# SyncE's issue of the expert blocks' quarter transfers: unrolled program against a loop of six blocks on the engine

## The chip, the cores and the metric

One core of one Trainium2 chip runs one program. The metric is the time on the device in microseconds (us), the median of several runs. All five engines work side by side, each through its own sequence of instructions; they meet at semaphores. SyncE (SP in the profile) computes nothing: it issues DMA transfers.

## The reference, cut to what matters

The computation is one layer over x of 32 sequences of 256 rows of 512 numbers: a cross attention with 16 heads whose result is added to x, and then a routed feed-forward product that is added as well. Only the second part is touched:

```python
scores = jnp.einsum('sp,tp->st', pe, jnp.sign(tile_sigs))
idx = jnp.argmax(scores, axis=-1)                    # one of 8 experts for each position
y_all = jnp.einsum('bsd,tod->bsto', x, W) + b
out = jnp.take_along_axis(y_all, idx4, axis=2)[:, :, 0]
x = x + out                                          # the x in the product is normalized
```

The expert depends on the position (0 to 255) alone, so all 32 sequences send the same position to the same expert.

## The kernel before, in words

Until about 700 us the kernel runs the attention, tile by tile. It leaves two arrays in HBM: `y_scratch` (the sum so far, plus the expert's bias) and `x_scratch` (the same rows normalized, in four column quarters). Then the expert stage begins. The 256 positions are sorted by expert and padded to 70 blocks (`NR`) of four positions (`PB`); four positions times 32 sequences are the 128 rows of a block. Which four positions block j holds is known only at run time; they stand in the small tile `position_of`.

For each block j five engines work:

- SP, in `gather_quarters`: it waits until the slot of `xq` is free (`x2t_ready` at least j - 5; there are R = 6 slots), reads the four positions of the block into registers (L1645, one TENSOR_LOAD), and issues four transfers of 64 KB from `x_scratch` (L1649). The source address of each comes from a register, which takes a FUSED_REGOPS and a MOVE ahead of each DMA. In the program before, j is a number of the program's text: the 70 blocks stand one behind the other, 280 transfers in all.
- DVE: it transposes the block from `xq` to `x2t` (L1698, two slots), computes the low part of x (L1703), and in `finish` adds the product to the gathered rows of y (L1711). A `finish` waits for the product, for the gathered rows and for an earlier scatter.
- ACT: it rounds `x2t` to its high part (L1688).
- PE: 12 matmuls of 128x512 a block (L1747), into two PSUM buffers in turn; a block waits for the `finish` of two blocks earlier (`y2_ready`). PE already runs its 70 blocks as a first turn of six in the program's text, a loop of ten turns of six blocks (`pe.Fori`, L1768), and four blocks at the end.
- POOL: an indirect gather of y rows (L1663), five blocks ahead, and an indirect scatter of the result (L1669), one of each a block, 256 KB each.

The order on each engine is written out by hand. Nothing but SP's own program and the freed slot holds back a quarter transfer.

Of the kernel before, what the change touches and what calls it, by code (L numbers as in the profile page):

```python
# [31 lines left out]
P = 128  # L32
B, S, DM = 32, 256, 512
# [11 lines left out]
PB = P // B  # L45
NR = (S + NE * (PB - 1)) // PB
# [18 lines left out]
def wait(eng, sem, value):  # L65

    if isinstance(value, int) and value <= 0:
        return
    eng.wait_ge(sem, value)
# [82 lines left out]
def kernel_program(nc, x, x_t, ctx_t, mask, pad, wq, wk, wv, wo, sigs_t, wf, bf, ident_d, choose_d, slots_d, place_d, pe_t, out):  # L152
# [4 lines left out]
    x_quarters = nc.dram_tensor("x_scratch", (KC * B, S, P), F32, kind="Internal").ap()  # L157
    top = ExitStack()
    with top:
        def sb(name, shape, dt=F32, stack=top):  # L160
            return stack.enter_context(nc.sbuf_tensor(name, shape, dt))

        def sem(name):
            return top.enter_context(nc.semaphore(name))
# [15 lines left out]
        position_of = sb("position_of", [1, NR, PB], I32)  # L180
# [1443 lines left out]
        R = 6  # L1624
        xq = sb("xq", [P, R, DM])
# [7 lines left out]
        quartered = [sem(f"quartered_{r}") for r in range(R)]  # L1633
        x2t_ready = sem("x2t_ready")
# [3 lines left out]
        y2_ready = sem("y2_ready")  # L1638
        scattered = [sem(f"scattered_{r}") for r in range(3)]

        def gather_quarters(eng, j, quarters):

            r = j % R
            wait(eng, x2t_ready, j + 1 - R)
            _, at = nc.values_load_multi_w_load_instructions(  # L1645
                position_of[0:1, j, quarters.start:quarters.stop], engines=[eng.engine], min_val=0, max_val=S - 1,
                skip_runtime_bounds_check_because="a position comes from a one-hot product with the numbers 0 to 255")
            for s, n in zip(at, quarters):
                eng.dma_start(xq[:, r, n * P:(n + 1) * P],  # L1649
                              x_quarters[:, bass.ds(s, 1), :].rearrange("p a f -> p (a f)")).then_inc(quartered[r], 16)  # L1650

        def experts_sync(sp):
            sp.wait_ge(positions_known, 1)
            for j in range(NR):
                gather_quarters(sp, j, range(PB))

        def experts_gpsimd(pool):
            last_row = pool.to_reg(B * S - 1)
# [115 lines left out]
        with nc.Block() as block:  # L1774
# [33 lines left out]
            @block.sync  # L1808
            def _(sp):
                either(sp, short_sync(sp, SHORT), full_sync)  # L1810
                experts_sync(sp)
# [92 lines left out]
```

## Time and profile before

| | |
|---|---|
| median of 3 runs | 945.48 us (943.81 to 946.06) |
| profiled execution, its own time | 945.56 us |
| its span in the trace | 943.7 us |
| granted TensorE clock, mean | 0.985 |
| busy: PE, PEld, DVE, POOL, ACT | 93%, 74%, 76%, 68%, 46% |
| SP's queue (q1) | 104.69 MB, 35.5% of 16 DMA engines' span |
| POOL's queue (q0) | 35.66 MB, 11.8% |

The span is what the trace covers; about 1.9 us of the execution's own time lie around it. Register, branch, semaphore and DMA-issuing instructions are not counted as busy. In rows an engine's name with a q is its sequencer (SPq, PEldq); "issue" in a chain is time in which the engine waited for nothing that the profile shows. The expert stage is the last quarter of the span, from 700 us on.

### The profile page before, as it was taken

How to read it: one execution, taken by the hardware profiler on the slowest of the kernel's cores; microseconds unless marked ns; L12 is line 12 of the kernel's file. 1: busy time of each engine (PE TensorE's matmuls, PEld its weight loads, DVE VectorE, ACT ScalarE, POOL GpSimd, SP SyncE). 2: the span in 40 equal slices, each digit the busy share in tenths (PEclk: the TensorE clock that was granted, in tenths of full speed). 3: DMA queues.
4: the chain of work that ended last, by engine and by line, in shares of the span. 5: the costliest groups of instructions: out<-in, count | busy, mean ns of one | idle time of the engine just before them, and what ended most of it. 6: DMA issues, size and time to landing. Idle time of an engine off the chain costs nothing.

```text
span 943.7 us, 16943 instructions
## 1 busy us (share of the span) xinstructions
PE 879.9 (93%) x5430; PEld 700.6 (74%) x5431; DVE 715.6 (76%) x1021; ACT 432.5 (46%) x762; POOL 640.2 (68%) x833
## 2 busy tenths in 40 slices
PE   6999999999999999999999999999927888888986
PEld 4788887887888788788878878887715666666765
DVE  5899778788887878888788888887757666666664
ACT  5545555565555556455545655553561212111211
POOL 3687777586676858767685866765674666666764
PEclk9999999999999999999999999999968999999999
DMA  9513242424324242532433243322876777778883
GB/s 347 179 35 121 71 145 82 125 78 148 117 75 144 83 125 69 158 97 96 133 93 125 69 158 82 110 70 79 290 249 199 237 236 239 242 242 243 249 247 116
DMA packets 123123, 141.59 MB, mean 150 GB/s; under 512 B 16128, under 2 KB 89376, under 8 KB 120992
## 3 DMA queue, kind: packets, MB, share of 16 engines
q1 hardware_dynamic: 111296, 104.69, 35.5%
q0 software_dynamic: 11360, 35.66, 11.8%
q8 instruction: 42, 0.69, 0.3%
q14 instruction: 41, 0.34, 0.1%
q10 hardware_dynamic: 384, 0.21, 0.1%
HBM read 90.18 MB, written 51.90 MB: 151 GB/s over the span
## 4 chain that ended last, share of the span: by engine, by line
PE 85%; issue 4%; SPq 3%; DMA 3%; DVE 2%; POOL 2%; ACT 1%; DVEq 0%; POOLq 0%; ACTq 0%
PE pS L1458 29%; PE pA L1458 19%; PE pA L1747 15%; PE pS L1524 7%; PE pA L1547 7%; PE pT L1535 6%; SPq L1649 2%; DMA x_scratch<-y_normal 1%; DMA xq<-x_scratch 1%; PE pS L1484 1%; DVE y L1711 1%; POOL wf_hl L321 1%; POOL y_biased L1057 1%; DVE wf_hl L321 1%; DVE x2t L1698 0%
## 5 line engine op out<-in xcount | busy, mean ns | idle before, releaser
L1747 PE MATMUL pA<-wf_hl,x_hi 128*128 x560 | 144.6, 401 | 40.6 <-DVE y L1711 22.3
L1747 PEld LDWEIGHTS pA<-wf_hl,x_hi 128*128 128x128 f32 x560 | 105.6, 191 | 71.0 <-issue 50.3
L1301 DVE TENSOR_TENSOR s<-pS,bias 128x1024 f32<-128x1024 f32 x57 | 69.3, 1217 | 75.9 <-PE pS L1524 75.9
L1688 ACT CAST x_hi<-x2t 128x512 fp32r<-128x512 f32 x70 | 43.4, 621 | 182.0 <-PE pA L1747 106.3
L1072 POOL TENSOR_TENSOR s<-s,row 128x1024 f32<-128x1024 f32 x64 | 121.7, 1902 | 4.5 <-DVE row L1321 4.5
L1669 POOL DMA_INDIRECT out_dram<-y,scatter_rows x70 | 79.6, 1138 | 63.7 <-DVE y L1711 48.8
L1188 ACT CAST ot_hi<-pA 128x512 fp32r<-128x512 f32 x64 | 37.6, 587 | 180.3 <-PE pA L1547 180.3
L1458 PE MATMUL pA<-wo_hi,ot_hi 128*128 128x512 f32 x256 | 108.8, 425 | 2.9 <-DVE ot_lo L1325 2.9
L1048 POOL TENSOR_SCALAR y_mom<-y_mom 128x1 f32<-128x1 f32 x64 | 13.8, 216 | 143.6 <-DVE y_mom L1341 142.1
L1458 PE MATMUL pS<-xt_hi,wq_hi 128*128 128x512 f32 x256 | 105.0, 410 | 2.3 <-DVE wq_lo L1361 2.3
L1458 PE MATMUL pA<-wo_hi,ot_lo 128*128 128x512 f32 x256 | 101.5, 396 | 0.0
L1458 PE MATMUL pA<-wo_lo,ot_hi 128*128 128x512 f32 x256 | 101.4, 396 | 0.0
L1458 PE MATMUL pS<-xt_hi,wq_lo 128*128 128x512 f32 x256 | 100.7, 393 | 0.0
L1458 PE MATMUL pS<-xt_lo,wq_hi 128*128 128x512 f32 x256 | 100.4, 392 | 0.0
L1032 POOL TENSOR_TENSOR xt_lo<-xt_raw,xt_hi 128x512 fp32r<-128x512 f32 x64 | 94.4, 1505 | 6.7 <-ACT xt_hi L1144 6.7
L1310 DVE SCALAR_TENSOR_TENSOR s<-row,s 128x1024 f32<-128x1024 f32 x57 | 95.2, 1670 | 1.9
L1663 POOL DMA_INDIRECT yg<-y_scratch,gather_rows x70 | 71.2, 1017 | 25.1 <-issue 16.8
L1711 DVE TENSOR_TENSOR y<-pA,yg 128x512 f32<-128x512 f32 x70 | 47.2, 674 | 51.6 <-PE pA L1747 48.7
L1057 POOL TENSOR_TENSOR y_biased<-y,bias_at 128x512 f32<-128x512 f32 x64 | 82.0, 1282 | 2.7 <-DMA x_scratch<-y_normal 2.7
L1316 DVE TENSOR_REDUCE row<-s 128x16 f32<-128x1024 f32 x64 | 76.0, 1188 | 3.2 <-ACT s L1178 2.9
L1178 ACT ACTIVATE s<-s,rstd 128x1024 f32<-128x1024 f32 x64 | 73.9, 1155 | 9.1 <-DVE s L1310 8.8
L1747 PE MATMUL pA<-wf_hl,x_lo 128*128 x280 | 75.1, 390 | 2.1 <-DVE x_lo L1703 2.1
(131 smaller groups left out, 1935.8 us busy)
## 6 DMA issues: line engine op xcount, KB each, us to landing
xq<-x_scratch SPq DMA_DIRECT2D x280, 64.0 KB
xt_raw<-in_x_t SPq DMA_DIRECT2D x16, 1024.0 KB, 6.8
x<-in_x SPq DMA_DIRECT2D x64, 256.0 KB, 3.2
y_scratch<-y_biased SPq DMA_DIRECT2D x64, 256.0 KB, 2.1
x_scratch<-y_normal SPq DMA_DIRECT2D x64, 256.0 KB, 2.8
wf_hl<-in_wf SPq DMA_DIRECT2D x8, 1024.0 KB, 8.5
ctx_raw<-in_ctx_t SPq DMA_DIRECT2D x32, 128.0 KB, 2.8
mask_early<-in_mask SPq DMA_DIRECT2D x1, 1536.0 KB, 11.3
```

Of the source, the lines that this page charges most:

```text
L1032: pool.tensor_tensor(h.xt_lo[:, k, :], h.xt_raw[:, k, :], h.xt_hi[:, k, :].bitcast(F32), ALU.subtract)\
L1057: pool.tensor_tensor(y_biased[:, t % 2, :], y_sb[:, t % 2, 0:DM], bias_at[:, t % 2, :], ALU.add)\
L1072: pool.tensor_tensor(p, p, h.row[:, t % h.c, 3, :].unsqueeze(2).broadcast_to([P, H, BK]), ALU.mult)\
L1178: act.activation(p, p, ACT.Exp, scale=h.rstd[:, t % h.c, 2:3]).then_inc(exp_ready, 1)
L1301: dve.tensor_tensor(h.s_sb[:, t % h.c, :].rearrange("p (h k) -> p h k", h=H), pS[:, 0, :].rearrange("p (h k) -> p h k", h=H), h.bias[:, t ...
L1310: dve.scalar_tensor_tensor(p, h.row[:, t % h.c, 0, :].unsqueeze(2).broadcast_to([P, H, BK]), FLOOR, p, ALU.max, ALU.subtract).then_inc(shi ...
L1316: dve.tensor_reduce(row[:, 1, :], h.s_sb[:, t % h.c, :].rearrange("p (h k) -> p h k", h=H), AX.X, ALU.add).then_inc(sum_ready, 1)
L1458: mm = pe.matmul(dst, lhs[a], rhs[b], start=(k == 0 and n == 0), stop=(k == KC - 1 and n == 2))
L1524: mm = pe.matmul(pS[:, 0, g2 * 512 + m * P:g2 * 512 + (m + 1) * P], h.qt[half, g % 2, m, q * P:(q + 1) * P], h.kd[half, g % 2, q // 2, m, ...
L1663: pool.indirect_dma_start(yg[:, r, :], None, y_rows, bass.IndirectOffsetOnAxis(ap=gather_rows[:, j:j + 1], axis=0))\
L1669: pool.indirect_dma_start(out, bass.IndirectOffsetOnAxis(ap=scatter_rows[:, j:j + 1], axis=0), y2[:, j % 3, :], None, bounds_check=last_ro ...
L1747: return pe.matmul(pA[:, r % 2, :], rows[:, r % 2, c * P:(c + 1) * P], w, start=first, stop=last)
```

## The change

`gather_quarters` takes a turn k and a place n in it, j = 6k + n, in place of j. Turn 0 (blocks 0 to 5) and the last four blocks (66 to 69) stay in the program's text; turns 1 to 10 (blocks 6 to 65) are a loop on SyncE whose body holds six blocks. In the body k is a register. So the address of the four positions and the value that `x2t_ready` is compared with are computed on the engine; the slot of `xq` and the semaphore of the transfer depend on n alone and stay constants. Which transfers are issued, how large they are, and in which order, is the same.

```diff
-        def gather_quarters(eng, j, quarters):
-
-            r = j % R
-            wait(eng, x2t_ready, j + 1 - R)
+        def gather_quarters(eng, k, n):
+
+            j = R * k + n
+            if not isinstance(k, int):
+                wait(eng, x2t_ready, R * k + (n + 1 - R))
+            elif k > 0:
+                eng.wait_ge(x2t_ready, j + 1 - R)
             _, at = nc.values_load_multi_w_load_instructions(
-                position_of[0:1, j, quarters.start:quarters.stop], engines=[eng.engine], min_val=0, max_val=S - 1,
+                position_of[0:1, j, :] if isinstance(j, int) else
+                position_of[0:1, bass.ds(j, 1), :].rearrange("a j n -> a (j n)"), engines=[eng.engine], min_val=0, max_val=S - 1,
...
-            for s, n in zip(at, quarters):
-                eng.dma_start(xq[:, r, n * P:(n + 1) * P],
-                              x_quarters[:, bass.ds(s, 1), :].rearrange("p a f -> p (a f)")).then_inc(quartered[r], 16)
+            for q, s in enumerate(at):
+                eng.dma_start(xq[:, n, q * P:(q + 1) * P],
+                              x_quarters[:, bass.ds(s, 1), :].rearrange("p a f -> p (a f)")).then_inc(quartered[n], 16)
 
         def experts_sync(sp):
             sp.wait_ge(positions_known, 1)
-            for j in range(NR):
-                gather_quarters(sp, j, range(PB))
+            turns = NR // R
+            for n in range(R):
+                gather_quarters(sp, 0, n)
+            with sp.Fori(1, turns) as k:
+                for n in range(R):
+                    gather_quarters(sp, k, n)
+            for n in range(NR - R * turns):
+                gather_quarters(sp, turns, n)
```

## Rows read from the trace of the kernel before

**Rows 1.** The page: chain that ended last, shares of the span.
```profile
PE 85%; issue 4%; SPq 3%; DMA 3%; DVE 2%; POOL 2%; ACT 1%; DVEq 0%; POOLq 0%; ACTq 0%
```

**Rows 2.** Waits from 700 us on: who <- for whom: us in total, times, longest us.
```profile
POOL out_dram L1669 <- DVE y L1711: 48.8, 22, 10.3
DVE y L1711 <- PE pA L1747: 48.7, 23, 3.8
PE pA L1747 <- DVE y L1711: 22.3, 15, 1.7
...
SPq L1645 <- DVE x2t L1698: 0.7, 3, 0.3
```

**Rows 3.** SP's loads of positions and DVE's transposes, 720 to 845: min/median/max ns, first to last start.
```profile
L1645 SPq TENSOR_LOAD <-position_of x37: 3/296/873, 722.0 to 843.7; - x37
...
L1698 DVE STREAM_TRANSPOSE x2t<-xq x39: 702/705/712, 722.5 to 842.2; 128x512 f32<-128x512 f32 x39
...
  DMA xq<-x_scratch: 3.7, 4
```

**Rows 4.** The same from 845 to 930.
```profile
L1645 SPq TENSOR_LOAD <-position_of x26: 3/298/822, 848.8 to 927.2; - x26
...
L1698 DVE STREAM_TRANSPOSE x2t<-xq x27: 702/711/715, 845.3 to 928.8; 128x512 f32<-128x512 f32 x27
...
  DMA xq<-x_scratch: 19.7, 18
```

**Rows 5.** Chain of waits, one block's head and first transfer on SP: start us, us, what.
```profile
837.25 0.30 SPq L1645
837.55 0.03 issue
837.58 0.04 SPq L1649
837.62 0.04 issue
837.65 0.03 SPq L1649
837.68 0.03 issue
837.71 0.33 SPq L1649
838.05 0.05 issue
```

**Rows 6.** Chain of waits, SP some 7 us later.
```profile
844.38 0.71 SPq L1649
...
845.11 0.70 SPq L1649
845.81 0.71 issue
...
846.53 0.70 SPq L1649
```

**Rows 7.** PE's own loop: its end (L1768) and the register work of a block.
```profile
L1768 PEldq FUSED_REGOPS  x10: 28/59/708, 731.4 to 903.9; - x10
L1768 PEldq ALU_OP  x10: 13/32/65, 750.8 to 921.8; - x10
L1768 PEldq COMPARE_BRANCH  x10: 3/208/247, 750.8 to 921.9; - x10
...
L1740 PEldq FUSED_REGOPS  x120: 3/151/700, 695.6 to 931.8; - x120
```

**Rows 8.** DMA queues from 745 to 925: packets, MB, share of 16 engines.
```profile
q0 software_dynamic: 9043, 29.25, 50.8%
q1 hardware_dynamic: 31462, 14.33, 28.5%
q14 instruction: 9, 0.07, 0.1%
```

**Rows 9.** The branch past the attention's other form, on SP and on PE.
```profile
L1802 SPq COMPARE_BRANCH  x2: 41/45/49, 35.1 to 702.7; - x2
L1802 PEldq COMPARE_BRANCH  x2: 95/2951/5807, 43.1 to 689.3; - x2
```

**Rows 10.** Chain of waits: a transpose that waited for its quarters, and the end.
```profile
848.84 0.30 SPq L1645
...
850.86 3.59 DMA xq<-x_scratch
...
854.47 0.72 DVE x2t L1698
...
929.23 2.88 DMA xq<-x_scratch
932.14 0.06 DVE x2t L1698
```

## The prediction

> **What bounds the kernel now.** The page's chain comes first: over the whole span it is PE's (85%), and SP's sequencer has 3% of it [rows 1]. That is an average; the change touches the last quarter alone, so the stage's own views decide. The waits from 700 us on show PE, DVE and POOL in a ring: PE waits for DVE's `finish` 15 times for 22.3 us, DVE for PE, POOL for DVE. SP waits for a free slot for 0.7 us in all 70 blocks [rows 2]. So SP is never held back by its consumers: it issues as fast as it can. The question is how near it is to being late.
>
> The loads of positions mark SP's start of each block, the transposes DVE's. From 720 to 845 SP starts 37 blocks, from 722.0 to 843.7: 121.7 / 36 = 3.38 us a block; DVE starts 39 in 119.7 us, 3.15 a block [rows 3]. The counts give the places: 70 - 37 - 26 = 7, so SP is at block 7 when DVE (whose last transpose, block 69, lies behind the second stretch [rows 10], so 70 - 39 - 27 - 1 = 3) is at block 3. At the end of that stretch it is 43 against 41. SP loses its lead, 0.23 us a block. From 845 on DVE waits for quarters 18 times for 19.7 us, against 4 times for 3.7 us before, and SP's pace is 78.4 / 25 = 3.14 us [rows 3, 4]. In the last third, then, SP's issue is what the stage waits for, and the last block's data land at 932.1, with nothing but that block's work behind them [rows 10].
>
> Why does SP need 3.14 to 3.38 us? A clean block costs 0.33 us for the load and 4 x (0.04 + 0.04 + 0.03 + 0.03 + 0.33 + 0.05) = 4 x 0.52 us, 2.41 in all [rows 5]. The rest, 0.97 us a block in the first stretch and 0.73 in the second, comes in spells like that of [rows 6], where steps that take 0.03 to 0.33 us otherwise follow each other at 0.70 us, whatever their kind. They fall into the time when both queues are full (together 79% of 16 engines) [rows 8]. I read this as contention, not as SP's own work; the trace doesn't show its place.
>
> **The change part by part.**
>
> *Transfers.* The same 280, in the same order, from the same registers: nothing.
>
> *Register work of a block in the loop.* Two instructions are added: one for the address of the positions, one for the value of the wait; the wait itself rides on an instruction as before. On SP a FUSED_REGOPS with its gap is 0.08 us and a MOVE 0.06 [rows 5]: 0.07 each, 0.14 a block. PE's program for the same thing (an address from 6k + n) has a FUSED_REGOPS of 0.15 us among its own [rows 7]; so the upper bound is two of those with gaps, 0.36 a block. The lower one is a single instruction, 0.07. I take 0.16, near SP's own rows.
>
> *The loop's end, once in six blocks.* SP has no such row. PE's is 0.03 + 0.21 + 0.06 us and some 0.10 of gaps, 0.40 [rows 7], 0.07 a block. Bounds: 0.05 us (SP's branch at L1802 takes 0.041 to 0.049 [rows 9]) and 0.7 (one step at the slow pace of [rows 6]), so 0.01 to 0.12 a block.
>
> *Code loading.* The unrolled blocks are read as they are run: 9 packets on the instruction queue q14 in 180 us, 0.1% of the engines [rows 8]. Removing them gives nothing that I can price: 0 to 0.5 us.
>
> Sum: 0.23 us a block in the clean case, 60 blocks, 13.8 us of SP's time. If the added instructions meet the slow spells as often as the others do, it is 0.23 x 3.38 / 2.41 = 0.32.
>
> *What of it reaches the end.* First it eats the lead. SP starts block 7 at 722.0, and at 3.38 + 0.32 = 3.70 a block it reaches block 21 at 773.8. DVE transposes block 7 four blocks behind block 3, at about 722.5 + 4 x 3.15 = 735.1, and block 21 at 779.2. The gap is then 5.4 us; when a transpose waited for its quarters it came 854.47 - 848.84 = 5.6 us after SP's load [rows 10]. So the lead is gone at block 21 in place of block 43 or so. From there 48 blocks go at SP's pace. Before, SP came to block 69 at 927.2 [rows 4]. After, at 773.8 + 48 x (3.14 + x), where x is what is left of the addition once SP sets the pace: x = 0 gives 924.5, which the ring of PE, DVE and POOL at 3.15 a block doesn't allow to help, so no change; x = 0.23 gives 935.6, +8.4 us; x = 0.32 gives 939.9, +12.7.
>
> How large is x? The two stretches are an experiment of their own. When SP began to set the pace, its slow time fell from 0.97 to 0.73 us a block: with consumers waiting, POOL issues less and the spells shorten. Part of an addition comes back that way. I take half of 0.32, x = 0.16: 773.8 + 48 x 3.30 = 932.2, which is 5.0 us later than 927.2, and all behind it moves along. Against the profiled execution's own 945.56: **950.6 us**. That execution lies 0.08 us from the median shown, so nothing is corrected.
>
> A page speaks against this change in a harder way. PE's loop turned ten times with a branch of 0.21 us at most 0.25 [rows 7], and no packet of another instruction queue than q14 is there from 745 to 925 [rows 8]. The Trainium skill, Runtime: NRT & Kernel Launch, section Instruction fetch mechanics, says that prefetch is purely sequential and that a taken branch whose target isn't in the two pages held forces a fetch before execution goes on. By that rule a body small enough for the pages costs nothing extra (by its 64-byte instructions SP's body of some 95 is about 6 KB, an estimate) and the sum stays; a body that doesn't stay resident gives the last rival below.
>
> **The rivals.**
>
> *The addition is absorbed.* The stage may be limited by what the queues carry, and SP's slow time is then only how it is told. For it: the 0.24 us that came back above, and DVE's pace, which moved little between the stretches. Against: DVE's 19.7 us of waits for quarters, which are SP's lateness. Time: x = 0, 945.6, give or take 2.
>
> *Faster.* SP runs up to four blocks ahead early on, and its transfers compete with POOL's gathers and scatters just when PE waits for `finish`. A slower SP spreads them: the spells in which everything is late get shorter, and PE's 15 waits for `finish` (22.3 us [rows 2]) shrink. If a quarter of it goes, 5.5 us: 940. It decides from the point where the spells end before DVE's `finish` is due, that is, if PE and not SP sets the pace after block 21. For it: SP's slow time fell as SP lost its lead. Against: the transfers are the same bytes in the same time, and DVE was waiting for quarters 18 times.
>
> *The branch back reloads code.* PE's far branch at 689.3 took 5.81 us, SP's own far branch at 702.7 0.04, with the next load of positions soon behind [rows 9]. Ten turns at 2 us (between the two) are 20 us, most of it on the path since the lead is gone by then: with the 5.0 above about 968. For it: only the page's rule and PE's one far branch. Against: PE's ten near branches.
>
> **How the numbers follow.** Forecast (some of the addition arrives, +3 to +13): 0.45. Absorbed: 0.30. Faster: 0.17. Reload: 0.08. The likeliest alone has 948.4 to 958.3. The range reaches to the faster and absorbed cases and above x = 0.32 with the upper bound of the register work: 941.5 to 960. A measurement of this kernel tells about 0.3%, 2.8 us, from no change. Faster by more than that: 0.17, and a little of the absorbed case, 0.18; within: 0.30; slower: 0.45 + 0.08 less what falls inside, 0.52.
>
> **What would show it.** In the trace after: two more register instructions a block on SP and a compare-and-branch ten times; a clean block of SP at 2.6 us instead of 2.41; SP's pace from 722 on near 3.7 and later 3.3; DVE's waits for quarters beginning near block 21, about 790 us, and growing well above 20 us in all; PE's waits for `finish` turning into waits for the high part or the transpose. The forecast is wrong if SP's clean block has not grown, if DVE's waits for quarters stay at 20 to 25 us, if a gap of over 1 us stands at each branch with packets on the instruction queue beside it, or if PE's matmuls run closer together than before.

## The result and the profile after

The changed kernel takes 950.06 us (median of 5, 947.54 to 954.71) against 945.18 us (median of 5, 943.75 to 946.06): a ratio of 1.0057, 95% interval 1.0039 to 1.0076. It is 4.9 us slower.

The profiled execution after is the slowest of its five, 954.71 us with a span of 952.8, so its trace has to be cut before it is compared. (Its mean granted clock is 0.978, where the profiled execution before has 0.985; the other four after have 0.982 to 0.984 and still take 947.54 to 952.23 us, so the clock is not the medians' difference.) The stage starts where SP loads the first positions. The first group below is that line in the trace after, in the form of [rows 3].

```profile
L1648 SPq TENSOR_LOAD <-position_of x70: 3/298/776, 706.4 to 935.8; - x70
L1648 SPq FUSED_REGOPS  x60: 3/60/719, 723.1 to 922.3; - x60
```

Before, the first load is at 703.2 (the first DMA of the stage follows at once) and the last at 927.2. So 3.2 of the 9.1 us between the two spans were lost before the expert stage, in code that the change doesn't touch; the stage itself went from 240.5 to 246.4 us, 5.9 more. SP's way from its first to its last block went from 224.0 to 229.4 us, 5.4 more. That is about the size of the medians' difference. All that follows on single blocks rests on one trace of each kernel.

The page's chain has turned over, compare [rows 1]:

```profile
PE 70%; SPq 15%; issue 8%; DMA 3%; POOL 2%; DVE 1%; ACT 0%; POOLq 0%; DVEq 0%; ACTq 0%
```

SP's sequencer has 15% of the span where it had 3. The waits from 700 us on (who <- for whom: us, times, longest us) answer to [rows 2]:

```profile
DVE x2t L1708 <- DMA xq<-x_scratch: 54.8, 39, 2.9
POOL out_dram L1679 <- DVE y L1721: 52.4, 29, 10.1
...
DVE y L1721 <- PE pA L1757: 28.3, 16, 3.8
PE pA L1757 <- ACT x_hi L1698: 26.5, 13, 16.7
...
PE pA L1757 <- DVE y L1721: 16.7, 11, 1.7
```

DVE's waits for quarters are 54.8 us, 39 times; PE now waits for the rounded x (without the one of 16.7 us, which is the start of the stage, 9.8 us in 12 times; before, once for 1.0 us from 720 on), and less for `finish` (16.7 us where it was 22.3). Where do they begin? Transposes of the trace after from 720 to 775, 775 to 845 and 845 to 940, each with its waits for quarters:

```profile
L1708 DVE STREAM_TRANSPOSE x2t<-xq x17: 702/705/711, 719.3 to 772.2; 128x512 f32<-128x512 f32 x17
...
  DMA xq<-x_scratch: 2.4, 2
...
L1708 DVE STREAM_TRANSPOSE x2t<-xq x21: 705/711/714, 776.2 to 841.9; 128x512 f32<-128x512 f32 x21
...
  DMA xq<-x_scratch: 18.7, 14
...
L1708 DVE STREAM_TRANSPOSE x2t<-xq x29: 703/711/714, 845.7 to 938.0; 128x512 f32<-128x512 f32 x29
...
  DMA xq<-x_scratch: 28.4, 21
```

From 775 to 845 the kernel before has 3.7 us of them in 4 waits (all of those in [rows 3]); here they are 18.7 in 14. That is the lateness which the kernel before has from 845 on [rows 4], some 70 us earlier.

The work added is seen in the chain, as the same stretch of a block as [rows 5] (start us, us, what):

```profile
775.84 0.04 SPq L69
775.87 0.03 issue
775.90 0.06 SPq L1648
775.96 0.04 issue
776.00 0.30 SPq L1648
776.30 0.03 issue
776.33 0.04 SPq L1653
...
778.39 0.04 SPq L69
```

An ALU_OP (L69, the line of the helper `wait`) computes the value of the wait (0.07 us with its gap), a FUSED_REGOPS the address of the positions (0.10); everything behind is as before. The clean block from 775.84 to 778.39 takes 2.55 us, where it took 2.41. The FUSED_REGOPS is there in each of the 60 blocks of the loop, the ALU_OP only in 40 of them:

```profile
L69 SPq ALU_OP  x40: 4/37/689, 725.6 to 919.7; - x40
```

So the register work added is 0.17 us in two blocks of three and 0.10 in the third, 0.15 in the mean. The loop's end, and a stretch some six us later in which most steps take 0.7 us:

```profile
765.46 0.04 SPq L1661
765.49 0.04 issue
765.53 0.04 SPq L1661
765.58 0.21 issue
765.78 0.23 SPq L1661
...
771.97 0.67 SPq L1653
772.69 0.69 SPq L69
773.42 0.03 SPq L1653
773.45 0.65 issue
```

The branch back costs 0.04 and a gap of 0.21 us, once in six blocks; and the added L69 takes 0.69 us when it meets a slow spell, 17 times what it takes otherwise.

### The profile page after: what moved, and what is told of

It is laid out like the page before. It is cut to its first block, busy times and chain, and to the rows that moved or that the text cites. A ratio compares the mean times of both kernels' runs of the same rounds, so it can differ in the third digit from the quotient of the medians.

```text
span 952.8 us, 17075 instructions
## 1 busy us (share of the span) xinstructions
PE 885.6 (93%) x5430; PEld 702.6 (74%) x5431; DVE 715.4 (75%) x1021; ACT 432.9 (45%) x762; POOL 643.8 (68%) x833
## 4 chain that ended last, share of the span: by engine, by line
PE 70%; SPq 15%; issue 8%; DMA 3%; POOL 2%; DVE 1%; ACT 0%; POOLq 0%; DVEq 0%; ACTq 0%
PE pS L1458 29%; PE pA L1458 19%; SPq L1653 11%; PE pS L1524 7%; PE pA L1547 6%; PE pT L1535 5%; SPq L1648 3%; PE pA L1757 2%; DMA x_scratch<-y_normal 1%; PE pS L1484 1%; DMA xq<-x_scratch 1%; POOL wf_hl L321 1%; SPq L310 1%; POOL y_biased L1057 1%; DMA wk_raw<-in_wk 0%
## 5 line engine op out<-in xcount | busy, mean ns | idle before, releaser
L1679 POOL DMA_INDIRECT out_dram<-y,scatter_rows x70 | 83.2, 1188 | 65.9 <-DVE y L1721 52.4
L1708 DVE STREAM_TRANSPOSE x2t<-xq 128x512 f32<-128x512 f32 x70 | 49.6, 709 | 58.2 <-DMA xq<-x_scratch 54.8
```

The costliest lines, as they stand in the source:

```text
L1679: pool.indirect_dma_start(out, bass.IndirectOffsetOnAxis(ap=scatter_rows[:, j:j + 1], axis=0), y2[:, j % 3, :], None, bounds_check=last_ro ...
```

## The experiments

Theory A: what costs is the time that the loop adds to SyncE's issue of each block, and only where that issue is what the stage waits for. Rivals: B, the loop as such costs; C, the queues set the pace and absorb SyncE's time; E, a branch back over a long body reloads code. Of the slow steps: F, they are what full queues look like, against G, they come from outside the program. All comparisons are with the kernel before in the same set of runs. That matters, because the kernel before doesn't take the same time in every set: 945.2 us in the pair above and 946.8 in the set with the copies, but 916.4, 915.9 and 916.1 us in the three others. Within a set it is steady (35 executions from 914.8 to 919.7 us in one of them). The two are called the 945 us condition and the 916 us condition here. The runs were spread over chips: number 6 for the register additions and the first split, number 1 for the increments and the thirty blocks, number 5 for the copies, and number 5 again, some six minutes later, for the last run. Chip 5 has 946.8 us in the one set and 916.1 in the other, so the chip's number does not tell which condition a set is in.

**Register additions, two and eight a block.**

```diff
+            if R <= j < NR - NR % R:
+                for _ in range(2):
+                    eng.reg_add(spare, spare, 1)
```

> The program of before, unrolled, with two register additions ahead of each block's load of positions, for blocks 6 to 65. Theory A (SyncE's instructions per block are the cost, not the loop): 2 x 0.07 us x 60 = 8.4 us of SyncE's time in the clean case, against 13.8 that I reckoned for the loop; by the same working the time goes up by about 3 us (ratio 1.002 to 1.005), and a clean block of SyncE takes 2.55 us. Rival B (the loop itself costs: the branch, the code behind it, the waits on a register): no change, ratio 0.998 to 1.001.

> The same with eight register additions a block: 8 x 0.07 = 0.56 us a block clean, 33 us of SyncE's time. Theory A with nothing absorbed: the pace of SyncE from 720 us on is 3.14 + 0.56 = 3.7 us a block, +28 to +33 us (ratio 1.030 to 1.035). Theory A with half absorbed, as in the prediction: +15 us (1.013 to 1.020). Rival B: no change. Rival C (queues set the pace, all absorbed): under +5 us (1.005).

Measured: 0.9996 (0.9984 to 1.0008) and 1.0000 (0.9991 to 1.0008), 916.1 and 916.3 us against 916.4. They say nothing on the dose: nobody read the register, and the additions aren't in the traces. They are two copies of the kernel before, and as such useful. First the stretch from 760 to 800 in the kernel before, then in the first of the copies (busy us with counts by engine, granted clock, DMA share, GB/s):

```profile
760.00:800.00 40.00, 34.97 (x150) 28.12 (x151) 25.55 (x40) 7.97 (x14) 26.67 (x25) 1.00 0.78 237
```

```profile
760.00:800.00 40.00, 40.00 (x178) 33.10 (x177) 29.93 (x45) 9.23 (x15) 31.16 (x30) 1.00 0.93 289
```

The same program, the same clock of 1.00: in the 916 us condition TensorE is busy 40.00 of 40 us and the queues carry 289 GB/s at 0.93 of their time, in the other 34.97 us, 237 GB/s and 0.78. PE's own check of its expert number (SEQ_ASSERT, min/median/max ns) shows what is missing; before, the loop of the first pair, and the copy:

```profile
L1740 PEldq SEQ_ASSERT  x70: 3/18/697, 695.8 to 932.0; - x70
```

```profile
L1750 PEldq SEQ_ASSERT  x70: 3/18/707, 699.1 to 941.2; - x70
```

```profile
L1746 PEldq SEQ_ASSERT  x70: 18/18/26, 695.3 to 901.1; - x70
```

An instruction of 18 ns takes up to 707 in the one condition and never over 26 in the other. The slow steps are not SyncE's alone: TensorE's sequencer has them too. And they are absent where the queues are fuller, 0.93 against 0.78 of their time, so rival F falls here: full queues do not make them.

**Half of the quarters issued by ScalarE, SyncE unrolled and in a loop.**

```diff
             for j in range(NR):
                 high(j)
+                if j + R < NR:
+                    act_quarters(act, j + R)      # quarters 2 and 3; SyncE issues 0 and 1 from block 6 on
```

> Unrolled, but from block 6 on ScalarE issues quarters 2 and 3 of each block, right behind its rounding of the block six earlier; SyncE issues 0 and 1. SyncE's clean block falls from 2.41 to about 1.35 us. Theory A: DVE's waits for quarters (19.7 us from 845 on in the kernel before) go away and the stage is set by the ring of TensorE, VectorE and GpSimd: 0 to 5 us faster (ratio 0.995 to 1.000). Rival C: no change. Rival D (ScalarE's issuing delays its roundings): slower, ratio over 1.003.

> The changed program (loop of six blocks on SyncE), with quarters 2 and 3 issued by ScalarE from block 6 on as in the run before this one. Theory A: SyncE now has over 1 us to spare in each block, so the loop costs nothing: the same time as the unrolled split within 0.2%. Rival B: it is slower than the unrolled split by the same 0.5% by which the loop is slower than the kernel before.

Measured: 1.0008 (0.9996 to 1.0019) and 0.9997 (0.9987 to 1.0007). Here SyncE isn't late in the first place, so there was nothing to win and nothing to lose. ScalarE's issuing does no harm in this condition (rival D of that run is out). On theory A against C these two runs say nothing.

**The changed kernel again, and a dose that stays in the program.**

> The changed kernel itself, once more. In the runs so far the kernel before took 916.4 us in place of 945.2, and SyncE's steps of 0.70 us were absent from its expert stage: SyncE's clean block of 2.41 us stood against TensorE's 2.72 us a block. Theory A (the loop costs only what it adds to SyncE's issue, and only where that is what the stage waits for): clean block 2.57 us with the loop, still under 2.72, so no change if those conditions hold again (ratio 0.999 to 1.001), and 1.004 to 1.008 if the slow steps are back. Rival B (the loop itself costs, wherever it runs): 1.005 in both.

```diff
+            if R <= j < NR - NR % R:
+                for _ in range(2):
+                    eng.sem_inc(tick, 1)
```

> Unrolled, with two increments of an unused semaphore on SyncE ahead of each load of positions, blocks 6 to 65; no loop. (The register additions of the first two runs were not in the program that ran: their traces have no such instruction, so they were copies of the kernel before.) About 0.06 us each, clean block about 2.53 us. Theory A: with SyncE's slow steps absent no change (0.999 to 1.001); with them as with the loop, 1.003 to 1.007. Rival B: no change in either.

> The same with eight increments, clean block about 2.9 us. Theory A: with the slow steps absent SyncE becomes the bound at 2.9 against 2.72 us, after its lead of four blocks is used up: (60 x 0.18) less about 5 us of lead, +5 us (ratio 1.003 to 1.012); with them +15 to +30 us. Rival C (the queues set the pace and absorb SyncE's time): no change.

Measured: the loop 1.0010 (0.9999 to 1.0021), 916.1 against 915.9 us; two increments 1.0000 (0.9991 to 1.0009); eight 1.0205 (1.0179 to 1.0230), 933.3 us. The loop costs 0.5% in the 945 us condition and at most 0.2% in this one, which rival B has no place for. Eight increments without any loop cost 17.3 us, and two of them nothing: a threshold, as theory A wants. Of the traces, SyncE's loads of positions from 760 to 900 in the copy of before and with eight increments, and DVE's waits for quarters from 720 to 900 with the loop:

```profile
L1650 SPq TENSOR_LOAD <-position_of x47: 295/567/943, 762.1 to 887.6; - x47
```

```profile
L1650 SPq TENSOR_LOAD <-position_of x46: 294/300/908, 760.5 to 899.5; - x46
```

```profile
  DMA xq<-x_scratch: 0.3, 1
```

SyncE goes from 125.5 / 46 = 2.73 to 139.0 / 45 = 3.09 us a block; with eight increments DVE waits 43.6 us for quarters from 720 to 900. I had expected 5 us, from a clean block of 2.9 against TensorE's 2.72. The mean was 3.09, and 0.37 a block over 60 blocks less the 5 us of lead is the 17 us. The slip was to reckon with the clean block in place of a pace such as was measured. Rival C is out for this condition.

The loop is not far from costing something here either. In the copy of before VectorE starts to transpose block 21 12.5 us after SyncE has started to load its positions; with the loop it is 7.1 us, and from there to the end 6.4 to 7.5. A transpose that waited came 5.6 us behind [rows 10].

**Thirty blocks in the body.**

```diff
-            with sp.Fori(1, turns) as k:
-                for n in range(R):
-                    gather_quarters(sp, k, n)
+            with sp.Fori(0, 2) as k:
+                for n in range(30):
+                    gather_long(sp, k, n)     # j = 30 k + n + 6, otherwise the same
```

> The loop with 30 blocks in its body and two turns, in place of six and ten: one branch back over some 450 instructions. Theory A: as the loop of six within 0.1% (the branch is 0.07 us a block of the addition). Rival E (a branch whose target is no longer held reloads code): one stop of 1 to 6 us at that branch with packets on the instruction queue beside it, hidden in SyncE's lead if the slow steps are absent.

Measured: 1.0013 (0.9999 to 1.0026). The total hardly shows it, the trace does. First the loop's end with 30 blocks (x2: the branch is taken at 800.7, and the next instruction of the loop starts at 805.1) and the instruction queue from 800 to 806; then one end of the loop of six in the same set:

```profile
L1672 SPq FUSED_REGOPS  x2: 50/53/56, 719.4 to 805.1; - x2
L1672 SPq ALU_OP  x2: 37/39/41, 800.6 to 888.7; - x2
L1672 SPq COMPARE_BRANCH  x2: 44/49/54, 800.7 to 888.8; - x2
```

```profile
q14 instruction: 2, 0.02, 1.3%
```

```profile
L1661 SPq COMPARE_BRANCH  x1: 45/45/45, 753.4 to 753.4; - x1
L1661 SPq FUSED_REGOPS  x1: 50/50/50, 753.6 to 753.6; - x1
```

4.4 us against 0.25. The branch back over 30 blocks loads code; beside the one over six, from 753 to 755, there is no packet on an instruction queue. Rival E has its stop. It was taken once: of the two compares the second, at 888.7, leaves the loop. The stop used up what lead SyncE had: DVE waits for quarters 29 times for 22.8 us from 806 on, and not once from 720 to 800.

**Copies added to the stage.**

```diff
                 high(j)
+                if R <= j < NR - R:
+                    act.dma_start(copies[j * P:(j + 1) * P, :], x[j * P:(j + 1) * P, :]).then_inc(copied, 16)
```

> The kernel before with traffic added to its expert stage: for 58 of the 70 blocks ScalarE issues a copy of 128 rows of x (256 KB) from HBM to HBM into an array that nothing reads. It is to bring back, where the expert stage runs at TensorE's pace (2.72 us a block, the kernel before at 916 us), the condition of the first pair of runs (3.2 us a block, steps of 0.70 us on SyncE). One quarter more bytes on DMA engines that are 93% busy: I expect 3.1 to 3.4 us a block, some 945 us. Theory F (the slow steps are what full queues look like): steps of 0.70 us in SyncE's chain. Rival G (they came from something outside this program): longer landings, but no such steps, and SyncE's pace is held down by its DMA instructions alone.

> The changed kernel with the same copies. Theory A together with F: SyncE is late again, and the loop is 0.3 to 0.8% slower than the unrolled program with the same copies. Rival C (full queues absorb SyncE's time, the loss of the first pair came from another thing): the two are equal within 0.2%.

> The unrolled program with the same copies and with quarters 2 and 3 issued by ScalarE. Theory A: if SyncE's issue is what the loaded stage waits for, halving it makes this one faster than the unrolled program with the same copies, by 0.3 to 1%. Rival C: equal, since the bytes are the same.

These were meant for the 916 us condition and ran in the other, where the kernel before takes 946.8 us. So the copies didn't bring the slow steps back, they were added to them, and the forecast of some 945 us for the first of the three has no meaning. Measured, against the kernel before: unrolled 1.0177 (1.0154 to 1.0200), 964.1 us; loop 1.0257 (1.0234 to 1.0281), 970.7 us; unrolled with the issue split 1.0075 (1.0057 to 1.0093), 953.2 us. The loop costs 1.0257 / 1.0177 = 1.008, the split brings 0.990, with the same bytes. No execution of one overlaps the next: the split ends at 955.75 us, the unrolled program has 959.17 to 964.86, the loop begins at 968.24. DVE's transposes from 760 to 930 and their waits for quarters, unrolled, loop, split (the last has no such wait):

```profile
L1703 DVE STREAM_TRANSPOSE x2t<-xq x49: 704/711/716, 761.0 to 925.8; 128x512 f32<-128x512 f32 x49
...
  DMA xq<-x_scratch: 52.2, 38
```

```profile
L1713 DVE STREAM_TRANSPOSE x2t<-xq x47: 704/711/714, 761.6 to 929.1; 128x512 f32<-128x512 f32 x47
...
  DMA xq<-x_scratch: 66.0, 37
```

```profile
L1715 DVE STREAM_TRANSPOSE x2t<-xq x52: 698/705/709, 761.7 to 929.4; 128x512 f32<-128x512 f32 x52
```

That is 3.43, 3.64 and 3.29 us a block. Rival C falls here too: the queues would have carried the blocks faster, had the quarters been asked for sooner. Part of the difference can be TensorE's granted clock, which is 1.00 from 730 to 930 with the split, 0.83 from 800 to 810 in the unrolled program, and with the loop 0.83 from 770 to 780 and 0.66 from 920 to 930, at the lower of its two levels for a part of each. Around these falls TensorE had waited for the rounded x: 3.9 us from 785 to 804 in the unrolled program, 2.8 from 755 to 776 and 3.5 in one wait from 915 to 924 with the loop. The stretch from 760 to 800 with the copies, unrolled:

```profile
760.00:800.00 40.00, 35.62 (x149) 27.25 (x149) 22.59 (x35) 7.00 (x12) 28.02 (x25) 1.00 0.97 306
```

It moves 306 GB/s, where the kernel before moves 237 in the first pair and 289 in the 916 us condition, the last without slow steps. So it is not the number of bytes that decides whether they are there. Rival G is not shown by that; all that the runs say for it is that the same program has the steps in one set of runs and not in another.

The run with copies and split shows one thing more. In it SyncE and ScalarE issue quarters side by side, through the same two register instructions ahead of each transfer (SyncE's, then ScalarE's, min/median/max ns):

```profile
L1651 SPq FUSED_REGOPS  x152: 3/37/721, 703.0 to 922.8; - x152
L1651 SPq MOVE xq<-x_scratch x152: 3/29/965, 703.1 to 922.9; - x152
...
L1660 ACTq FUSED_REGOPS  x128: 37/37/42, 710.6 to 924.2; - x128
L1660 ACTq MOVE xq<-x_scratch x128: 29/29/41, 710.7 to 924.3; - x128
```

SyncE's take up to 0.72 and 0.97 us, ScalarE's never over 0.042. So the slow steps are on SyncE's and TensorE's sequencers and not on ScalarE's, and the split can help in two ways at once: SyncE has half of the work, and the other half is issued where there are no slow steps. No run tells the two apart.

**The split once more, without copies.**

> The unrolled program with quarters 2 and 3 issued by ScalarE, no copies: the candidate that may beat both kernels. Where the kernel before takes 916 us it was the same (1.0008). Where the kernel before takes 945 us, theory A says: DVE's waits for quarters (30 us in the trace of before, from 700 us on) go, the ring of TensorE, VectorE and GpSimd at 3.15 us a block stays, with its own slow steps: 2 to 8 us faster, ratio 0.991 to 0.998. Rival C: 1.000. If the kernel before takes 916 us again the run says nothing new.

Measured: 1.0001 (0.9991 to 1.0011), 916.1 against 916.1 us. It ran in the 916 us condition, where SyncE isn't late, and says nothing new. Whether the split beats both kernels where the loop costs 0.5% isn't measured; with the copies it beats the unrolled one by 1.0%. The 945 us condition without copies has only the first pair: neither a dose nor the split was measured in it. What shows the cause there are its two traces; the runs that vary SyncE's work are in the other condition or have the copies.

## Why the prediction was right

*Forecast 950.6 us, measured 950.06; +5.0 us against +4.9.* The mechanism is the one named: SyncE's own instructions, its lead used up, the rest passed on. The loop as such is not the cause (it costs at most 0.2% where SyncE has time) and eight increments without a loop do the same and more. That the two numbers lie 0.1 us apart is luck: the five executions after spread from 947.54 to 954.71, and two errors in the working cancel, as shown below.

*The addition.* 0.16 us a block and 0.07 for the loop's end were taken. In the trace after it is 0.15 in the mean (two instructions in 40 blocks, one in 20, where two were reckoned for all 60) and, from the loop's ALU_OP at 765.46 to the next address at 766.04, 0.58 / 6 = 0.10, with one step of 0.23 in it. The upper bound from PE's rows wasn't needed.

*The lead is gone at block 21.* The working had SP at block 21 at 773.8, 70.6 us into the stage. The loads of positions of the two traces, before from 768 to 770 (block 21) and after from 775 to 777 (block 21):

```profile
L1645 SPq TENSOR_LOAD <-position_of x1: 682/682/682, 769.1 to 769.1; - x1
```

```profile
L1648 SPq TENSOR_LOAD <-position_of x1: 301/301/301, 776.0 to 776.0; - x1
```

After it is 776.0 - 706.4 = 69.6 us, before 769.1 - 703.2 = 65.9: 3.7 us lost, where 14 x 0.32 = 4.5 were reckoned. Of the 3.7, 0.6 were lost before block 7, which SyncE loads at 725.8 after and 722.0 before; from block 7 to block 21 it is 50.2 against 47.1 us, 3.59 against 3.36 a block. That is an addition of 0.22, the clean sum, and not 0.32: the stretching by slow steps isn't seen. The lead is gone where the working had it: VectorE starts on block 21 5.5 us after SyncE's load (8.3 before), and its waits for quarters begin there.

*The pace from there on.* I took 48 x 3.30; the trace has (935.8 - 776.0) / 48 = 3.33. This term came out near by luck, for the pace of 3.14 under it was wrong: that is the pace of the last 25 blocks alone. Before, the same 48 blocks took (927.2 - 769.1) / 48 = 3.29. An x of 0.16 on top of that would have been 48 x 0.16 = 7.7 us; put on 3.14 it gave 0.5. What the traces show is 0.04 a block, 1.7 us in all. So of the addition of 0.23 to 0.32 us a block a sixth or less got through after block 21, not half; most was absorbed. From block 21 to 43, where SyncE before still had lead to lose, its pace is 3.39 before and 3.38 after; in the 26 blocks from there on it is 3.21 and 3.29. What absorbs the addition isn't shown. The two errors, a lead reckoned to lose 4.5 us that lost 3.7, and 0.5 us for the rest that was 1.7, nearly cancel: 5.4 against 5.0.

*The rivals.* Absorbed: true for most of the added time after block 21, and not for the whole, since 5.4 us do arrive, and the runs with copies show 0.8% for the loop and 1.0% for the split. Faster, by shorter slow spells: PE's waits for `finish` did fall, from 22.3 to 16.7 us, but its waits for the rounded x, 9.8 us, took their place. Reload: the loop of six doesn't, the loop of thirty does, with 4.4 us where the rival had 2 a turn. It had its mechanism right and the place wrong. The Trainium skill, Runtime: NRT & Kernel Launch, section Instruction fetch mechanics, ties the stop to a target outside the two pages held; the traces agree, 0.25 us a branch for the 91 instructions of the body of six blocks and 4.4 us with two packets for the 427 of the body of thirty.

*Not foreseen.* That the cost hangs on a condition outside the program. All numbers of the prediction came from a trace in which SyncE's and TensorE's sequencers have steps of 0.7 us; where they are absent the loop is within 0.2%. The prediction read these steps as contention at full queues, and fuller queues without them (0.93 against 0.78) speak against that.

## What to carry to other kernels

Before code on an issuing engine is changed, ask how far ahead of its consumers that engine is, and whether the lead shrinks: SyncE waited for nobody in the kernel before and was at its consumers' heels by block 43, so 0.2 us of register work a block came out in the time. In these runs a loop on SyncE costs its address and wait arithmetic and 0.25 us for the branch with a body of 91 instructions; the one branch back over 427 stopped it for 4.4 us. Where the issue is the bound, share it with an engine that has time: half of the quarters on ScalarE took 11 us off the stage with copies and made no difference where SyncE wasn't late. And measure a change beside the kernel before in the same set of runs: the condition here is worth 30 us, the change 5.

## What the hardware showed that I had not expected

The same program takes 945 us in one set of runs and 916 in another, 3% apart, and nearly all of it is in the last quarter: SyncE's first load of positions is at 703.2 us in the one trace and at 702.4 in the copy's. TensorE is busy 34.97 of 40 us there and 40.00 here, at the same granted clock. The mark of the slower condition is that instructions of 18 to 37 ns take 0.67 to 0.71 us on TensorE's and SyncE's sequencers, while the same kind on ScalarE's takes 42 ns at most. It isn't the number of bytes: the stage moved 289 GB/s without the steps, and 237, or 306 with the copies, with them. It isn't the chip by its number either, since chip 5 stands in the record with both conditions. What causes the steps stays open; no run here could switch them on or off. Register arithmetic whose result nobody reads isn't in the program that runs, so a dose has to be made of something that has an effect, such as an increment of a semaphore.
